# Second layer's V projection with tokens as rows: 4 matmuls of 128 x 128 and 16 copies in place of 64 matmuls of 32 x 32 and 4 copies

## What is computed

```python
    x = x + _L0_attn_a_ref(_layernorm(x, axis=-1), ...)
    x = x + _L0_ffn_ref(_layernorm(x, axis=-1), ...)
    x = x + _L0_attn_b_ref(_layernorm(x, axis=-1), ...)
    x = x + _L0_ffn_ref(_layernorm(x, axis=-1), ...)

    def _L0_attn_b_ref(x, w_tor, b_tor, in_proj_w, in_proj_b, out_w, out_b):
        S, B, E = x.shape                      # 16, 256, 128
        xt = x @ w_tor.T + b_tor
        qkv = xt @ in_proj_w.T + in_proj_b
        q, k, v = jnp.split(qkv, 3, axis=-1)
        ...                                    # 16 heads of 8
        scores = jnp.einsum('bhqd,bhkd->bhqk', q * scale, k) + bias
        attn = jax.nn.softmax(scores, axis=-1)
        o = jnp.einsum('bhqk,bhkd->bhqd', attn, v)
        ...
        return o @ out_w.T + out_b
```

## Time and profile before

| what | us |
|---|---|
| median of 3 runs | 886.98 |
| lowest and highest run | 883.74, 887.29 |
| span of the profiled execution | 926.2 |
| TensorE matmul busy | 746.1 (81%) |
| ScalarE busy | 524.2 (57%) |
| VectorE busy | 505.9 (55%) |
| GpSimd busy | 363.0 (39%) |

### The profile page before, as it was taken

The page is one execution under the profiler, slowest core; times in us unless marked ns, Lnnn a source line. Parts: engine busy times, 40 slices in busy tenths (PEclk is TensorE's granted clock), DMA queues, the critical chain, the costliest instruction groups (busy, mean ns, idle before and its releaser), DMA issues. The chain is left out here.

```text
span 926.2 us, 27043 instructions
## 1 busy us (share of the span) xinstructions
PE 746.1 (81%) x8818; PEld 600.2 (65%) x8819; DVE 505.9 (55%) x1787; ACT 524.2 (57%) x1016; POOL 363.0 (39%) x446
## 2 busy tenths in 40 slices
PE   1688887786179999999967898877629999999970
PEld 1356655455158888888834677666518888888860
DVE  3366876653435555555527565454435555555534
ACT  0589975652056666666617986643116666666630
POOL 0454764536713333333333114447642333333330
PEclk9989987885589999999999997997659999999985
DMA  6134011011211111111135000111121111111117
GB/s 193 38 98 121 22 40 36 25 31 56 75 39 48 46 46 46 49 49 46 38 107 172 11 4 24 30 33 41 40 72 40 48 49 47 46 46 46 49 33 268
DMA packets 53546, 54.45 MB, mean 59 GB/s; under 512 B 8192, under 2 KB 43008, under 8 KB 53472
## 3 DMA queue, kind: packets, MB, share of 16 engines
q1 hardware_dynamic: 41024, 31.61, 12.2%
q0 software_dynamic: 8640, 18.11, 6.0%
q10 hardware_dynamic: 3808, 3.70, 1.2%
HBM read 29.51 MB, written 23.86 MB: 58 GB/s over the span
## 5 line engine op out<-in xcount | busy, mean ns | idle before, releaser
L1656 POOL DMA_INDIRECT expert_out<-moe_b_out,moe_b_place x71 | 68.0, 957 | 145.3 <-DVE moe_b_out L1812 145.3
L1656 POOL DMA_INDIRECT expert_out<-moe_a_out,moe_a_place x71 | 68.0, 958 | 145.1 <-DVE moe_a_out L1812 145.1
L1688 PE MATMUL wide<-wgu,moe_b_hi 128*128 x284 | 94.9, 415 | 0.0
L1688 PE MATMUL wide<-wgu,moe_a_hi 128*128 x284 | 94.3, 413 | 0.0
L1069 POOL DMA_INDIRECT routed<-stream,lb_place x64 | 62.3, 974 | 63.1 <-PE wide L1117 18.5
L479 POOL DMA_INDIRECT routed<-stream,la_place x64 | 63.2, 987 | 42.9 <-DVE la_place L784 26.2
L1704 PE MATMUL wide<-wd,moe_a_hidT 128*128 x568 | 75.5, 276 | 1.4 <-DVE moe_a_out L1812 0.7
L1704 PE MATMUL wide<-wd,moe_b_hidT 128*128 x568 | 75.4, 276 | 1.3 <-DVE moe_b_out L1812 0.7
L1704 PEld LDWEIGHTS wide<-wd,moe_b_hidT 128*128 128x128 f32 x568 | 69.0, 192 | 2.2 <-issue 2.2
L1704 PEld LDWEIGHTS wide<-wd,moe_a_hidT 128*128 128x128 f32 x568 | 69.0, 192 | 2.2 <-issue 2.0
L1763 ACT ACTIVATE moe_b_glow<-wide 128x512 f32<-128x512 f32 x71 | 42.6, 599 | 44.1 <-PE wide L1688 44.0
(11 more groups left out here) (282 smaller groups left out, 1778.3 us busy)
## 6 DMA issues: line engine op xcount, KB each, us to landing
moe_a_rows<-routed SPq DMA_DIRECT2D x71, 67.0 KB
moe_b_rows<-routed SPq DMA_DIRECT2D x71, 67.0 KB
lb_outs<-expert_out SPq DMA_DIRECT2D x8, 512.0 KB
la_stage<-in_wg SPq DMA_DIRECT2D x8, 256.0 KB, 2.6
la_stage<-in_wu SPq DMA_DIRECT2D x8, 256.0 KB, 3.2
wd<-in_wd SPq DMA_DIRECT2D x8, 256.0 KB, 3.8
kept<-stream SPq DMA_DIRECT2D x8, 256.0 KB
lb_kept<-kept SPq DMA_DIRECT2D x8, 256.0 KB
```

Source lines behind the costliest of these rows:

```text
L1656: pool.indirect_dma_start(d.expert[:, :], bass.IndirectOffsetOnAxis(ap=place[s % 4][:, 0:1], axis=0), out[u][:, :], None).then_inc(stored[ ...
L1688: last = nc.tensor.matmul(ps[u][:, :], x[u][:, :], w(j, part), start=i == 0, stop=i == 2)
```

## The change

V is now projected with tokens as rows: for each tile of 128 tokens one matmul, whose weight operand is the tile of `xT` and whose moving operand the whole of `k.wv[1]`. In `psX` block b of a tile then has its tokens at partitions 32 b, with all four groups of heads side by side. `out_v` therefore copies 16 times, for each group j and block b from partitions 32 b to partitions 32 j, a piece of 4 tiles x 4 heads x 8 values.

```diff
-                for tb in range(4 * BATCH):
-                    for j in range(4):
-                        last = nc.tensor.matmul(
-                            psX[BLK * j:BLK * (j + 1), tb * 32:(tb + 1) * 32], xT[c % 2][:, tb * BLK:(tb + 1) * BLK],
-                            k.wv[1][:, j * 32:(j + 1) * 32], start=True, stop=True, tile_position=(0, BLK * j))
+                for t in range(BATCH):
+                    last = nc.tensor.matmul(psX[:, t * P:(t + 1) * P], xT[c % 2][:, t * P:(t + 1) * P], k.wv[1][:, :],
+                                            start=True, stop=True)
                 last.then_inc(v_ready, 1)
...
                 for j in range(4):
-                    rows = slice(BLK * j, BLK * (j + 1))
-                    last = nc.scalar.activation(
-                        stand[c % 2][rows, :, :, :, j * (HD + 1):j * (HD + 1) + HD].rearrange("p t b i e -> p (t b) i e"),
-                        psX[rows, :].rearrange("p (t i e) -> p t i e", i=4, e=HD), ACT.Copy)
+                    for b in range(4):
+                        values = psX[BLK * b:BLK * (b + 1), :].rearrange("p (t g i e) -> p t g i e", t=BATCH, g=4, e=HD)
+                        last = nc.scalar.activation(
+                            stand[c % 2][BLK * j:BLK * (j + 1), :, b, :, j * (HD + 1):j * (HD + 1) + HD],
+                            values[:, :, j, :, :], ACT.Copy)
                 last.then_inc(v_out, 1)
```

## The result

The changed kernel is a little slower: 892.49 us, median of 20 runs (886.36 to 896.35), beside 886.18 us for the kernel before, timed in turn with it (20 runs, 877.74 to 892.08). The ratio is 1.0068, 95% interval [1.0047, 1.009], which is +6.0 us. The forecast was 886.5 us and "within 0.5%" as the likeliest; the range 876 to 899 holds the time, the sign is that of rival B.

A forecast was written before the change was run, and what follows sets the result against it. The first half of the second layer was taken as bound by ScalarE, the second by TensorE. +6.0 us for quads 0 to 3 and -6.5 us for quads 4 to 7 gave -0.5 us on 886.98, so 886.5 us, range 876 to 899.

The forecast's parts named there:

- rival B: ScalarE decides: V's gaps shorter without the profiler, or moved into mixing; quads 4 to 7 +1.0 each, 897 us; chance 0.31.
- I make the sum as a difference inside this span and carry it to the median one to one: Whole kernel: changes summed in the 926.2 us profiled span apply unscaled to the 886.98 us median, 39.2 us lower.
- Quads 4 to 7: -6.5 us: Second half of the second layer: V's stall goes, 3.16 to 1.05 us; -1.5 for quads 4 to 6, -2.0 for 7.
- The gain that the sum put at nothing: Mixing in the first quads: the sum counts no stall removed there, only V being 0.25 us a quad shorter.
- Quads 0 to 3: +6.0 us: First half of the second layer: longer ScalarE copies, less the slack, cost 2.4 + 1.7 + 0.7 + 1.2 us.
- that wait does not end last: TensorE before project_k: its wait for v_out is covered, since turn_back before it waits for the later flat copy anyway.
- The end of the layer: GpSimd's last sends, 34.4 us, stay; timing follows the places of quad 5, with 3.99 us of wait to gain.
- 2.5 us more a quad: V copies on ScalarE: 16 at 0.315 us without overlap take 5.04 us against 2.53, 20 us over eight quads.
- V at 1.05 us: V projection on TensorE: one piece of 1.05 us in every quad, with no "issue" gap inside.
- Seven or eight packets fewer: Instruction queue q8: its packets fall by 7 or 8.
- Records down by 1920: TensorE's matmul and weight load records: 240 a quad go, 1920 in all.
- Rival C: Faster: small copies overlap, or a lost packet border also removes a stall of mixing; about -7 us, 880 us; chance 0.31.

The follow-up runs named there:

- before_again: The kernel before, unchanged, profiled a second time; the profiled execution took 946.47 us.
- before_third: The kernel before, unchanged, for a third profile; 935.7 us.
- after_again: The changed kernel, unchanged, timed again beside the kernel before at 936.44 us; 937.15 us, ratio 0.9997.
- matmuls_only: The kernel before with the new 4 V matmuls a quad but its 4 old copies, output wrong; 937.29 us, ratio 0.9931 to the kernel before.
- before_fourth: The kernel before, unchanged, profiled a fourth time, in a group where it takes 892.04 us; 891.02 us.
- matmuls_only_3: Third run of the kernel before with 4 V matmuls and the 4 old copies, output wrong; 877.06 us, ratio 0.9896 beside the kernel before at 892.04.
- matmuls_twice: The kernel before with its 64 V matmuls a quad issued twice to the same place; 970.71 us, ratio 1.0382 to the kernel before.
- copies_12_4: The changed kernel with 12 of its 16 copies a quad on ScalarE and 4 on VectorE; 879.87 us, ratio 0.9891 to the kernel before.
- late_sends_before: The kernel before with GpSimd's 64 sends of the second layer held back to its end; 975.83 us, ratio 1.0455 to the kernel before.

## Why the prediction was right or wrong

- **"I make the sum as a difference inside this span and carry it to the median one to one".** The stalls of this span are not those of the timed runs. The kernel has two levels: in groups of runs at 886 to 892 us, and at 935 to 942. In either, the profiled execution's own time is 2.2 us above its span (891.02 for 888.8, 935.7 for 933.5). So the span of the earlier trace rows, 926.2 us beside a median of 886.98, reads as no cost of the profiler but as an execution near the other level, whose single runs go down to 928.1; the highest single run of the kernel before at the first is 895.6. The 39 us were in sight, and the prediction even named them a doubt.
- **"Quads 4 to 7: -6.5 us".** This is the step that failed: it takes V's stall of 3.16 us for time that TensorE gets back, 2.1 us a quad. TensorE gets it back at neither level. At 886 to 892 us V takes 1.5 to 1.8 us in these quads, but for one gap in quad 7, and there is little to give back: from the V of quad 4 to that of quad 7 the kernel before needs 46.4 us and the changed one 48.5, +2.1. At 935 to 942 us the stall is there in two more traces, 3.2 us and more, but with the fewer matmuls it stands in the mixing instead: TensorE's "issue" idle time from the V of quad 4 to that of quad 7 is 11.3 and 10.7 us in before_again and before_third and 11.2 in after_again. That the ratio there is 0.9997, as the sum has it, is luck as far as this term goes.
- **The gain that the sum put at nothing.** What the fewer records do take away at both levels are the "issue" gaps of mixing between the V of quad 0 and that of quad 4: 3.5 to 4.0 us in the four traces of the kernel before, none in those of the changed kernel and of the three matmuls_only. From the V of quad 0 to that of quad 4 the kernel before takes 56.9 to 61.7 us, the three matmuls_only 52.5 to 53.2.
- **"Quads 0 to 3: +6.0 us".** 61.7 us before (before_fourth), 66.9 after, +5.3. The sum is near, the parts are not: in matmuls_only_3 this stretch takes 52.5 us, so by these traces the matmuls gave 9.2 us and the copies, with the half clock behind them, took 14.4.
- **"that wait does not end last"**, said of project_k and v_out. In quads 0 and 1 it does: TensorE idles 2.14 and 1.79 us before project_k for the V copies, in the changed kernel and the same in after_again (2.14 and 1.81).
- **The end of the layer.** The sum hung it on the places of quad 5 and 3.99 us of wait. At 886 to 892 us GpSimd does not wait for places at all, before or after; in the changed kernel its last wait is for TensorE's scores and ends at 591.4 us.
- **"2.5 us more a quad".** The mechanism was right, fixed cost and no overlap; the size was off: 16 copies take 4.59 and not 5.04 us, 0.278 each and 0.287 from one to the next, so +2.06. The Trainium skill's ScalarE: Activation LUTs ("What ACT_TABLE_LOAD costs") would have given an estimate of 186 + 128 x 0.833 = 293 ns for one, close to the 278 measured; the overlap of 93 ns that it gives for neighbours is not there between these copies.
- **V at 1.05 us** in one piece: 1.06 in five quads, up to 1.92 in quad 0 at half clock. **Seven or eight packets fewer**: 46 for 53. **Records down by 1920**: the page's instructions fall by 1824, which is 1920 less the 96 added copies.
- **Rival B** gave +10 us and what it needs: "the gaps in V are shorter", and TensorE "waiting more for ScalarE could also fall to 1.2 GHz for longer". Both came at this level; +6.0 us and not +10, among other things as a quad of the second half cost 0.7 and not 1.0. Its other way, that the gap leaves V and falls into mixing, came at 935 to 942 us. Its chance of 0.31 was too low for a trace whose span was 4.4% off the runs.
- **Rival C** had one half right: the lost records take stalls of mixing away, in the quads without sends, and without the copies this is worth about 1% (matmuls_only_3). The copies use it all up.
- The Trainium skill's Runtime: NRT & Kernel Launch ("Instruction fetch mechanics") has crossings into a new block mostly hidden. If the gaps are such crossings, the changed kernel at 890 us agrees, with no gap in V or mixing; the kernel before does not (1.87 us above), and at 937 us neither does the changed one, with 0.5 us gaps in rows of four.

What stays open: what sets the level. It lies in the two attention layers alone (the first ends its sends at 229 to 232 us or at 253 to 261, while the time from there to the second layer's first norm is 228 to 231 us at either level, and that from its last send to the end 239 to 242, in the seven traces of the two kernels), its sign is the number of gaps in bursts of small matmuls, and it held through each group. In the second layer holding the sends back takes most of them away, so the sends are part of it; why they disturb TensorE at one level and not at the other is not shown. That the gaps are waits for instructions is argued from the packets, matmuls_twice and the late sends, not shown directly; a kernel with the same records at shifted block borders was not run.

## What to carry to other kernels

Compare the profiled span with the timed runs before any stall is counted: where it lies 4% off, its stalls may not be in the runs, and the sum should be made for both cases. A stall that is removed from one burst can stand in the next one, so count the idle time of the whole stretch. Work added to an engine that another one waits for costs the idle time of that other one, and about as much again where the clock falls behind it (3.3 us for 1.60 in quad 3 here, 1.6 us for the same in quad 5); so split such work until the idle time is short (0.45 us here) instead of moving it whole. When a change saves on one engine and pays on another, time the two halves alone: here the saving was worth about 1% (in a kernel whose output is wrong, built for its time), the price took it and 0.7% more, and with a quarter of the copies on another engine the 1% was there.

## What the runs showed of the hardware

- The same kernel, in groups of 11 to 29 runs, stays at 886 to 892 us or at 935 to 942 us, also under one chip number.
- An idle time of 1.60 us on TensorE in quads 3 and 4 (17.6 us) was followed by 3.4 us at half the clock, the same idle time in quad 5 (15.6 us) by none, and one of 0.45 us in copies_12_4 (14.9 us) by none.
- GpSimd's indirect sends lengthen TensorE's stalls at the upper level: from the V of quad 4 to that of quad 7 the "issue" idle time is 10.7 us with them (before_third) and 1.2 without (late_sends_before), and the stretch takes 64.1 and 44.2 us.
- 2048 more records on TensorE came with 8 more packets on q8 (matmuls_twice).
- Copies of 32 x 128 from PSUM take 0.28 us on ScalarE and 0.29 on VectorE, and do not overlap on either: 16 of them 4.59 and 4.79 us, where 4 of 32 x 512 take 2.53.
